# An attention step meets the first expert tiles: tile list, routing and scatter in another order

## The reference

```
x = x + xattn(layernorm(x), ctx, ...)     # x, ctx: 32 sequences x 128 tokens x 256
x = x + ffn(layernorm(x), gate_w, w1, b1, w2, b2)

xattn (8 heads of 32, with gates):
  ig, fg = [q k v] @ w.T + b
  cs = cumsum(log_sigmoid(fg));  log_D = tril(cs_s - cs_t) + ig_t;  D = exp(log_D - max)
  C = (q k^T / sqrt(32)) * D;  h = C / (max(|sum C|, exp(-max)) + 1e-6) @ v
  norm of h by head, times out_w

ffn (8 experts, F = 1024, the best two of each token):
  gate_scores = softmax(xf @ gate_w);  top 2, renormalised
  y_e = gelu(xf @ w1_e + b1_e) @ w2_e + b2_e
  out = sum over the two chosen experts of score * y_e
```

## Time and profile before

| what | us |
|---|---|
| median of 3 runs | 683.49 (681.92 to 687.37) |
| profiled execution | 680.61 |
| its span on the core | 678.7 |
| TensorE busy | 632.4 (93%) |
| VectorE busy | 490.8 (72%) |
| ScalarE busy | 323.9 (48%) |
| GpSimd busy | 190.7 (28%) |

### The profile page before, as it was taken

The page is one execution under the profiler, slowest core; times in us unless marked ns, Lnnn a source line. Parts: engine busy times, 40 slices in busy tenths (PEclk is TensorE's granted clock), DMA queues, the critical chain, the costliest instruction groups (busy, mean ns, idle before and its releaser), DMA issues. The chain is left out here.

```text
span 678.7 us, 20377 instructions
## 1 busy us (share of the span) xinstructions
PE 632.4 (93%) x6738; PEld 537.1 (79%) x6739; DVE 490.8 (72%) x1330; ACT 323.9 (48%) x767; POOL 190.7 (28%) x185
## 2 busy tenths in 40 slices
PE   2799998999999878999999999999999999999985
PEld 2577777777777557889899898989888898988764
DVE  3458986999999965978889757576666767575662
ACT  3678877798897534364232323232332323232321
POOL 3000004143243431353363313232232313233212
PEclk9799997999999987999999999999999999999999
DMA  4443527475574444233357323231323233232100
GB/s 152 140 126 125 190 67 231 140 247 160 168 230 134 159 131 144 90 67 59 64 154 159 54 47 57 42 65 32 59 34 61 39 56 54 43 65 40 33 3 3
DMA packets 55037, 66.57 MB, mean 98 GB/s; under 512 B 5472, under 2 KB 50720, under 8 KB 54832
## 3 DMA queue, kind: packets, MB, share of 16 engines
q1 hardware_dynamic: 41552, 48.13, 24.2%
q0 software_dynamic: 13296, 17.32, 13.8%
q10 hardware_dynamic: 112, 0.08, 0.1%
HBM read 41.50 MB, written 24.92 MB: 98 GB/s over the span
## 5 line engine op out<-in xcount | busy, mean ns | idle before, releaser
L1035 ACT ACTIVATE decay_slots<-scores,b_turned 128x256 f32<-128x256 f32 (+1 forms) x312 | 124.2, 453 | 252.8 <-PE scores L1512 249.5
L1512 PE MATMUL scores<-x_slots,w_halves 128*128 128x256 f16 (+1 forms) x1872 | 205.4, 266 | 0.7 <-issue 0.6
L1512 PEld LDWEIGHTS scores<-x_slots,w_halves 128*128 x1872 | 174.7, 98 | 24.5 <-issue 1.3
L640 POOL DMA_INDIRECT expert_rows<-xf_rows,slot_i x64 | 71.0, 1110 | 229.9 <-issue 104.3
L1526 PE MATMUL pv<-w_halves,decay_slots 128*128 x864 | 97.8, 273 | 0.0
L1526 PE MATMUL gate_bank<-w_halves,q_and_k_halves 128*128 x840 | 94.9, 273 | 0.1
L1526 PEld LDWEIGHTS pv<-w_halves,decay_slots 128*128 128x128 f16 x864 | 84.1, 98 | 10.6 <-issue 0.3
L663 POOL DMA_INDIRECT out_rows<-work,row_ids x35 | 55.5, 1587 | 129.3 <-DVE work L2103 102.3
L663 POOL DMA_INDIRECT out_rows<-v_centred_and_one,row_ids x36 | 56.6, 1572 | 122.9 <-DVE v_centred_and_one L2103 89.5
L1526 PEld LDWEIGHTS gate_bank<-w_halves,q_and_k_halves 128*128 128x128 f16 x840 | 81.9, 98 | 10.2 <-issue 0.5
L1250 PEld LDWEIGHTS pv<-v_centred_and_one,decay_slots 128*128 128x128 f32 x512 | 66.3, 201 | 1.8 <-issue 0.3
(11 more groups left out here) (257 smaller groups left out, 850.8 us busy)
## 6 DMA issues: line engine op xcount, KB each, us to landing
weight_stage<-in_L_ffn_w SPq DMA_DIRECT2D x32, 512.0 KB, 4.0
x_slots<-in_x SPq DMA_DIRECT2D x16, 512.0 KB, 4.8
weight_stage<-expert_rows SPq DMA_DIRECT2D x30, 272.0 KB, 3.2
ctx_slots<-in_ctx SPq DMA_DIRECT2D x8, 512.0 KB, 6.0
out_rows<-x_slots SPq DMA_DIRECT2D x8, 512.0 KB, 5.2
v_centred_and_one<-expert_rows SPq DMA_DIRECT2D x9, 272.0 KB, 3.1
expert_rows<-v_centred_and_one SPq DMA_DIRECT2D x9, 272.0 KB
expert_rows<-xf_rows,slot_i POOLq DMA_INDIRECT x64, 3.8
```

The lines of the kernel that those rows point to most:

```text
L640: pool.indirect_dma_start(table, bass.IndirectOffsetOnAxis(ap=sloti[:, step[1], j, k:k + 1], axis=0), xfn[:, step[1], j, :], None, bounds_ ...
L1035: ins = act.activation(hf[:, f * R:f * R + tr.rows(0)], ps_s[:, q, n * R:n * R + tr.rows(0)], ACT.Gelu, bias=b1T[:, bass.ds(expert, 1), f] ...
L1512: ins = pe.matmul(o, w, xh[:, tr.slot(0) % 2, b, k, 0:tr.rows(0)], start=(n == 0), stop=(n == 3 * KC - 1))
```

## The change

It reorders. `early_counts` and `early_list` run in the last `body`, before `c_of(7,2)`; `x1_guess(6)` goes behind `decay(7,3,1)` on ScalarE, and all four `x1_normed(6)` behind `h_out(7,2)`. `turn_xf(6,0)` leaves the place before tile 0's row transposes; the routing of step 6 is spread over TensorE's turns 0, 1 and 2, and that of step 7 is one turn later, in 4 and 5. `choose(6)` and `x1_stats(7)` stand inside VectorE's turn 1, `records(6)` and `x1_norm(7)` inside turn 2, between the rows of the next tile and the gelu splits. On GpSimd the three credits are given at the kernel's first instruction, step 6's scatter goes behind the adds of tiles 0 and 1, and that of step 7 and the late lists one turn later. Two streams fewer stand before `times_v(7,2)`. No computation is added or dropped. In the diff below the tail of ScalarE's list goes on as before with each turn's number one higher; VectorE's `early_counts`, `early_list` and `c_of(nxt, 2)` stand in `body` behind `weights_low(nxt, 3)`, the loop over `beside` in `turn` behind `row_fields(tr, 1)`, and `records(last)`, `late_list0`, `1` and `2` behind turns 5, 6, 7 and 8.

```
@@ gpsimd
+                pool.sem_inc(s_af, FREE0)
...
                 run_steps(body, pool)
-                pool.sem_inc(s_af, FREE0)
...
-                scatter(NEXT_LAST)
                 pool.wait_ge(s_pv, (NSTEP - 1) * SB)
                 pool.memset(zeros, 0.0).then_inc(s_zero, 1)
                 pool.wait_ge(s_xo, 16 * EARLY_STEPS)
-                for n in range(1, 6):
+                for n in range(1, 3):
+                    add_rows(Turn(0, n))
+                scatter(NEXT_LAST)
+                for n in range(3, 7):
                     add_rows(Turn(0, n))
                 scatter(LAST)
-                for n in range(6, EARLY):
+                for n in range(7, EARLY):
@@ scalar
                     if step is not None:
-                        x1_guess(step)
+                        if after is not None:
+                            x1_guess(step)
...
                 sixth, last = NEXT_LAST, LAST
-                x1_normed(sixth, 0)
                 h_out(last, 1)
-                x1_normed(sixth, 1)
                 decay(last, 3, 1)
+                x1_guess(sixth)
                 h_out(last, 2)
-                x1_normed(sixth, 2)
+                for j in range(SB):
+                    x1_normed(sixth, j)
+                h_out(last, 3)
                 xf_turned(sixth, 0)
-                x1_normed(sixth, 3)
-                h_out(last, 3)
                 xf_low(sixth, 0)
-                xf_turned(sixth, 1)
-                xf_low(sixth, 1)
                 h_guess(last)
-                second_gate(sixth)
                 for_gelu()
                 act.wait_ge(s_tl, 2)
-                turn(Turn(0, 0), True, NT)
+                expert = act.value_load(exi[0:1, 0:1], min_val=0, max_val=NE - 1)
+                gelu(Turn(0, 0), expert, 0, True)
+                xf_turned(sixth, 1)
+                gelu(Turn(0, 0), expert, 1, True)
+                gelu(Turn(0, 0), expert, 2, True)
+                xf_low(sixth, 1)
+                gelu(Turn(0, 0), expert, 3, True)
+                turn(Turn(0, 1), False, NT)
                 for_exp()
+                second_gate(sixth)
                 x1_guess(last)
                 for_gelu()
...
@@ tensor
-                stream_before(last, 2, 5)
+                stream_before(last, 2, 3)
                 times_v(last, 2)
-                turn_xf(sixth, 0)
                 pe.wait_ge(s_tl, 2)
                 pe.wait_ge(s_ee, NSTEP * (2 * SB))
                 turn_rows(Turn(0, 0), 0)
-                xf_left(sixth, 0)
                 stream_before(last, 3, 3)
                 times_v(last, 3)
-                tile_turn(Turn(0, 0), True, NT, ((turn_xf, sixth, 1), (xf_left, sixth, 1), (logits, sixth), (ranks, sixth)))
+                tile_turn(Turn(0, 0), True, NT, ((turn_xf, sixth, 0), (xf_left, sixth, 0), (turn_xf, sixth, 1)))
...
-                for n in range(1, 3):
-                    tile_turn(Turn(0, n), False, NT)
-                tile_turn(Turn(0, 3), False, NT, ((turn_xf, last, 0), (xf_left, last, 0), (turn_xf, last, 1),
+                tile_turn(Turn(0, 1), False, NT, ((xf_left, sixth, 1), (logits, sixth)))
+                tile_turn(Turn(0, 2), False, NT, (None, (ranks, sixth)))
+                tile_turn(Turn(0, 3), False, NT)
+                tile_turn(Turn(0, 4), False, NT, ((turn_xf, last, 0), (xf_left, last, 0), (turn_xf, last, 1),
                                                   (xf_left, last, 1), (logits, last)))
-                tile_turn(Turn(0, 4), False, NT, (None, None, (ranks, last)))
+                tile_turn(Turn(0, 5), False, NT, (None, None, (ranks, last)))
@@ vector
                 def records(step):
-                    if g == EARLY_STEPS:
-                        early_counts()
...
+                    if nxt is not None and after is None:
+                        early_counts()
+                        early_list()
+                        c_of(nxt, 2)
                     if step is not None:
                         x1_stats(step)
...
+                    for routing in beside:
+                        routing[0](*routing[1:])
...
                 x1_norm(sixth)
-                c_of(last, 2)
-                early_list()
                 c_of(last, 3)
                 row_fields(Turn(0, 0), 0)
                 split_rows(Turn(0, 0), 0)
                 h_norm(last)
                 split_rows(Turn(0, 0), 1)
                 row_fields(Turn(0, 0), 1)
-                choose(sixth)
                 h_scaled(last)
                 h_weighted(last)
                 x1_of(last)
                 for q in range(4):
                     split_gelu(Turn(0, 0), q)
-                records(sixth)
-                x1_stats(last)
                 dve.wait_ge(s_b2, 16)
-                turn(Turn(0, 1), False, NT)
-                x1_norm(last)
-                turn(Turn(0, 2), False, NT)
+                turn(Turn(0, 1), False, NT, ((choose, sixth), (x1_stats, last)))
+                turn(Turn(0, 2), False, NT, ((records, sixth), (x1_norm, last)))
                 turn(Turn(0, 3), False, NT)
+                turn(Turn(0, 4), False, NT)
                 choose(last)
...
```

More of the change, by code:

```diff
@@ L1071, in _ @@
+                gelu(Turn(0, 0), expert, 2, True)
+                xf_low(sixth, 1)
+                gelu(Turn(0, 0), expert, 3, True)
+                turn(Turn(0, 1), False, NT)
                 for_exp()
+                second_gate(sixth)
                 x1_guess(last)
                 for_gelu()
-                turn(Turn(0, 1), False, NT)
+                turn(Turn(0, 2), False, NT)
                 for j in range(2):
                     x1_normed(last, j)
-                turn(Turn(0, 2), False, NT)
+                turn(Turn(0, 3), False, NT)
@@ L1078, in _ @@
                 for j in range(2, 4):
                     x1_normed(last, j)
-                expert = act.value_load(exi[0:1, 3:4], min_val=0, max_val=NE - 1)
-                gelu(Turn(0, 3), expert, 0, False)
+                expert = act.value_load(exi[0:1, 4:5], min_val=0, max_val=NE - 1)
+                gelu(Turn(0, 4), expert, 0, False)
                 xf_turned(last, 0)
-                gelu(Turn(0, 3), expert, 1, False)
+                gelu(Turn(0, 4), expert, 1, False)
                 xf_low(last, 0)
-                gelu(Turn(0, 3), expert, 2, False)
+                gelu(Turn(0, 4), expert, 2, False)
@@ L1086, in _ @@
                 xf_turned(last, 1)
-                gelu(Turn(0, 3), expert, 3, False)
+                gelu(Turn(0, 4), expert, 3, False)
                 xf_low(last, 1)
-                turn(Turn(0, 4), False, NT)
+                turn(Turn(0, 5), False, NT)
                 for_exp()
@@ L1092, in _ @@
                 for_gelu()
-                for n in range(5, EARLY):
+                for n in range(6, EARLY):
                     turn(Turn(0, n), False, NT)
@@ L2108, in gate_rows, with turn @@
                         dve.sem_inc(s_y, 1)
-                def turn(tr, first, left):
+                def turn(tr, first, left, beside=()):
                     if first:
@@ L2148, in _ @@
                     split_gelu(Turn(0, 0), q)
-                records(sixth)
-                x1_stats(last)
                 dve.wait_ge(s_b2, 16)
-                turn(Turn(0, 1), False, NT)
-                x1_norm(last)
-                turn(Turn(0, 2), False, NT)
+                turn(Turn(0, 1), False, NT, ((choose, sixth), (x1_stats, last)))
+                turn(Turn(0, 2), False, NT, ((records, sixth), (x1_norm, last)))
                 turn(Turn(0, 3), False, NT)
+                turn(Turn(0, 4), False, NT)
                 choose(last)
-                turn(Turn(0, 4), False, NT)
+                turn(Turn(0, 5), False, NT)
                 records(last)
-                turn(Turn(0, 5), False, NT)
+                turn(Turn(0, 6), False, NT)
                 late_list0()
-                turn(Turn(0, 6), False, NT)
+                turn(Turn(0, 7), False, NT)
                 late_list1()
-                turn(Turn(0, 7), False, NT)
+                turn(Turn(0, 8), False, NT)
                 late_list2()
-                for n in range(8, EARLY - 1):
+                for n in range(9, EARLY - 1):
                     turn(Turn(0, n), False, NT)
```

62 lines of the change are left out of this document (31 added, 31 removed).

## The result

| | median, us | ratio to before, 95% interval | profiled execution, us |
|---|---|---|---|
| before | 684.69 (4 runs) | | 680.61, span 678.7 |
| after | 673.09 (670.59 to 679.18, 4 runs) | 0.9859 [0.9817, 0.9902] | 674.40, span 672.2 |
| after, second call | 673.54 (6 runs) | 0.9841 [0.9787, 0.9895] | 677.95, span 676.0 |
| after, third call | 673.26 (6 runs) | 0.9839 [0.9793, 0.9886] | 675.01, span 672.8 |

The change makes the kernel faster by about 1.5%: 0.0141 x 684.69 is 9.7 us in the first call, and the other two give 10.9 and 11.0. Forecast were 13.0 us and 670.5, range 667 to 678. Two of the 29 executions of the kernel before in the second call took 1246 and 1582 us; they do not enter the ratios, which are of fast runs alone.

A forecast was written before the change was run, and what follows sets the result against it. TensorE's seam between attention and expert tiles bounds the end: 13.3 us lost, plus 0.4 for streams, less waits of 0.1, 0.25, 0.15 and 0.2, gives 13.0; 680.61 becomes 667.6, median 670.5 us, range 667 to 678.

The forecast's parts named there:

- The seam: Between the last attention step and the first expert tiles: TensorE starts turn 3 at about 280.2 us, not 293.27.
- The waits charged: TensorE waits left in the seam: 0.25 us for expert rows, 0.2 near the first gelus, 0.15 only in the sum.
- Lost: 13.3 us: Seam from 247.11 to 282.30 us: 35.2 us spent on 21.9 us of TensorE work at full clock.
- The clock's 7.0 us: Low granted clock behind TensorE's waits in the seam, costing 5.5 and 1.5 us on top of 6.2 idle.
- The 1.5 us of the second fall: Clock of 0.55 for 3.27 us from 269.73, behind the waits of 1.20 and 1.05 us; cost 1.5 us.
- The first fall, 5.5 us: Clock of 0.50 for 10.94 us from 251.06, behind the 3.95 us wait for expert rows; cost 5.5 us.
- Cost: nothing: Turn 5 behind the seam: VectorE's 4 us wait on GpSimd costs TensorE nothing, by 3.8 us.
- The GpSimd part: Step 6's scatter behind two adds: turn 3's wait goes, VectorE waits 4 us in turn 5, TensorE loses nothing.
- The table load: ScalarE before the first gelu: 1.28 us, gelu 0.01 us behind; the skill's 2.66 us would make the sum 12.1.
- The rivals: Short wait keeps the low clock, 0.15; list earlier but rows not, 0.08; slower through GpSimd's chain at turn 5, 0.05.
- GpSimd's cover of 3.8 us: Turn 5: VectorE's work behind its GpSimd wait ends at 322.4 us; TensorE wants it at 326.2.
- the first of them: Rival: a short seam wait stays and with it the low clock; gain 5.5 us, 678 us; chance 0.15.

The follow-up runs named there:

- e3: Changed kernel with the early list alone put back between c_of(7,2) and c_of(7,3): ratio to before 1.0015, median 684.62 us.
- e6: Changed kernel with the routing of step 6 back inside and right behind tile 0: ratio to before 0.9989, median 682.69 us.
- e8: Kernel before, unchanged, run again for a second profile: median 686.41 us (1 run), stretch from scores(7,3) to turn 3 48.5 us.
- e2: Kernel before with 16 unused stream matmuls where TensorE waited 3.95 us for the first expert rows: ratio to before 0.9946, median 681.83 us.
- e5: Changed kernel with step 6's scatter ahead of the adds of tiles 0 and 1 again: ratio to before 0.9986, median 683.34 us.
- e1: Changed kernel, unchanged, run again for a tighter interval and second profile: ratio to before 0.9841, median 673.54 us.
- e10: Changed kernel with ranks(7) a quarter later and the six streams before times_v(7,2) and times_v(7,3) left out: ratio to before 0.9862, median 666.99 us.
- e7: Changed kernel with choose(6), x1_stats(7) behind VectorE's turn 1 and records(6), x1_norm(7) behind turn 2, not inside: ratio to before 0.9888, median 676.30 us.
- e9: Changed kernel with ranks(7) one quarter later in TensorE's turn 5: ratio to before 0.9835, median 663.25 us.
- e12: Changed kernel, unchanged, a third time, on the same chip as the repeat with ranks(7) a quarter later: ratio to before 0.9839, median 673.26 us.
- e4: Changed kernel with GpSimd's three credits given after the scatter of step 5 again: ratio to before 0.9946, median 680.55 us.
- e11: Changed kernel with ranks(7) one quarter later in TensorE's turn 5, run again beside the changed kernel: ratio to before 0.9846, median 673.24 us.

## Why the prediction was right, and where it was not

**The seam, right in size and in steps.** Counted from `scores(7,3)`, which the prediction put at 243.1: turn 3 was forecast 37.1 us later and comes 37.15 later. The list, row loads and rows ("landing 246.5", 3.4 us later) come at 3.0; `c_of(7,3)` 3.35 and 3.03; the first gelu ends 13.4 and 13.7 us later; the add of tile 2 gives its credit 70.4 and 69.5 us later. The waits charged (0.25, 0.15, 0.2) became 0.29, for `h_out(7,2)` rather than for rows, and 0.43 with nothing shown; the 0.15 in the sum belongs to no wait that the working names. e3 and e6 show the two causes that the argument named, rows landing late and the wait for `choose`, each with the clock's fall behind it.

**"Lost: 13.3 us", right as an account of one execution, too large as a price.** It was made from the first profile of before, whose stretch of 50.2 is the longer of two; e8 has 48.5, with a wait of 3.4 instead of 3.95 and a clock of 0.89 over the stretch instead of 0.83. Against e8 the seam gains 11.4.

**The clock's 7.0 us as a term of its own, mis-sized.** The rows are right, the sum in them holds, and e2 shows that the clock alone gives 3.4 to 5.1 us of stretch and 3.7 us of time. The 1.5 us of the second fall were worth nothing: in e8 that turn ran at a clock of 1.00 and took as long (12.59 us against 12.57). The first fall, 5.5 us, was mostly real, but in e2 TensorE then waited longer for `choose` (1.79 us against 1.20). It is no term that adds to the wait's: with one of the two gone, TensorE meets the next wait. The parts undone one by one cost 11.9, 7.2, 9.9, 10.1 and 3.2 us, 42 together, of a gain of 11. Even with their intervals they are links of a chain, not shares of a sum.

**"Cost: nothing" for the turns behind the seam, wrong by about 1 us.** The GpSimd part of it was right. VectorE waits in turn 5, for 2.22 us rather than 4, TensorE doesn't, and e5 shows what the order was worth. What the step missed is the pause in `ranks(7)`, 0.9 to 1.5 us in turns 3 to 6, which the rows before could not show. Its cause is open. Behind turn 7 nothing was lost: what follows it takes 338.9 us before and 339.2 in e8, 339.5 after and 339.3 in e1.

**The table load.** The trace shows the load alone again, 1.28 us and a gelu 0.02 us behind it, so the Trainium skill's further 1.38 us (ScalarE: Activation LUTs, What ACT_TABLE_LOAD costs) did not come in here: the load begins when the activation ahead ends, at 259.7, and the gelu begins when the load does end. TensorE's 0.43 us before turn 1 came with the gelu of quarter 0 done 0.8 us before layer 1 of tile 1 began.

**The median.** 13.0, less 1 for the pause and up to 1.7 for the long profile, is 10.3 to 12; measured are 9.7 (6.7 to 12.5 by its interval), 10.9 and 11.0 by the ratios. So the gain was forecast 2 to 3 us too large, and all three lie under the 11.5 to 14 that the sum allowed for it; the range of the median held, as it reached further up. Of the 2.6 us by which 673.1 lies over 670.5, 1.2 are the median of before, 684.7 rather than 683.49. The rivals did not come: the clock stayed at 1.00, the list was what SyncE waited for, GpSimd's cover of 3.8 us held. e10 shows how near the first of them was: a wait of 1.41 us was followed by a clock of 0.50 there, though one of the same length was not in e7.

## What to carry to other kernels

Walk the seam between two stages forward from one fixed event, engine by engine, with the time at which each result is there and the time at which it is wanted; the slack that comes out tells which moves must be made together, and undoing a single one can give back nearly all. Price a low clock behind a wait by what the other engines allow at full clock, not by its length alone, and look at filler matmuls twice before taking them out. Take the price of a loss from two executions at least, and compare stretches that begin at the same event, since what comes before may differ by more than the change is worth.

## What the runs showed that I had not expected

- The attention steps of the same code ended at 243.0, 250.3 and 253.0 us in three executions, and those of the changed kernel at 248.1, 251.6 and 249.1; in the call of e9 and e10 at 237.4 and 237.5. Their lengths go with the clock granted in them, 0.99 on average in e9 and e10, 0.95 or 0.96 in the two executions of before and the first one after, 0.94 in e1 and e12, 0.93 in e2; why it differs from one execution to the next is open. Timed runs of one kernel in one call spread by up to 10 us, nearly as much as the change gives.
- Waits of much the same length did and did not lower the clock. After 1.41 us (e10) it was 0.50, and after 1.20 and 1.05 (before) 0.55; after 1.41 (e7), after 1.79 and 1.05 (e2), and after 1.21 and 1.05 in the second execution of the very kernel before (e8) it stayed at 1.00. What decides was not settled.
- TensorE can pause 0.4 to 1.1 us in the middle of 16 small matmuls or right behind them with no wait shown. It did so in `ranks(7)` in each of the three profiles of the changed kernel and in e3 and e4, not in e5, e6 and e7, which have these matmuls in the same place, and not when they stand a quarter later (e9 to e11). Its cause is open; that instructions arrive late there is a guess that no run tested.
